# Delta rule and mixture of a six-stage decoder: when small triangular inverses are turned between layouts, and how keys and norms are interleaved

## The reference

```python
combine = combine.at[jnp.arange(N)[:, None], topk_idx].add(topk_scores)
hidden = silu(einsum('nd,kde->nke', flat, gate)) * einsum('nd,kde->nke', flat, up)
out = einsum('nk,nkd->nd', combine, einsum('nke,ked->nkd', hidden, down))
out = out + (silu(flat @ sh_gate.T) * (flat @ sh_up.T)) @ sh_down.T
```

```python
K = K / max(norm(K), EPS); beta = sigmoid(x @ Wbeta + b_beta)
def step(W, inp):
    pred = einsum('bhij,bhj->bhi', W, k_t)
    W_new = W + b_t * einsum('bhi,bhj->bhij', v_t - pred, k_t)
    return W_new, einsum('bhij,bhj->bhi', W_new, q_t)
```

## Time and profile before

| what | value |
|---|---|
| median of 3 runs | 1878.89 us |
| lowest, highest | 1873.01, 1880.94 us |
| the profiled execution | 1880.19 us, its span 1878.4 us |
| busy share of the span | PE 86%, DVE 62%, ACT 49%, POOL 34% |
| mean granted clock of PE | 0.914 of full speed |
| mixture, about | 990 to 1185 us of the span |
| delta rule, about | 1185 to 1700 us |

### The profile page before, as it was taken

One profiled execution on the slowest core, in us unless ns is written; L12 is line 12 of the kernel. 1 busy time (PEld: TensorE's weight loads), 2 busy tenths in 40 slices (PEclk: granted clock), 3 DMA queues, 4 the chain that ended last, 5 costly groups with the idle time before them and its releaser, 6 DMA issues.

```text
span 1878.4 us, 41473 instructions
## 1 busy us (share of the span) xinstructions
PE 1622.5 (86%) x17930; PEld 847.8 (45%) x17930; DVE 1168.0 (62%) x2285; ACT 912.0 (49%) x1263; POOL 646.1 (34%) x696
## 2 busy tenths in 40 slices
PE   4888887778998999899888987898988889878995
PEld 1222222223334334333434544676767778664443
DVE  6778775776575665657516567456464665455655
ACT  1665564456875775677571332344444443223120
POOL 1000000245654664565470007545665456000000
PEclk8897898899999999999997998799998999977898
DMA  3000002222242222242301000000000000100000
GB/s 138 1 1 1 1 1 76 65 66 66 80 105 66 77 80 66 66 105 77 80 10 60 3 1 1 13 14 14 3 14 14 14 14 21 47 2 1 6 6 12
DMA packets 31271, 69.91 MB, mean 37 GB/s; under 512 B 4954, under 2 KB 6047, under 8 KB 30832
## 3 DMA queue, kind: packets, MB, share of 16 engines
q1 hardware_dynamic: 31088, 67.26, 12.4%
HBM read 46.73 MB, written 20.51 MB: 36 GB/s over the span
## 4 chain that ended last, share of the span: by engine, by line
PE 65%; DVE 25%; issue 5%; ACT 4%; DMA 1%; POOL 1%; SPq 0%; DVEq 0%; ACTq 0%
PE ps L158 63%; DVE a_MX L362 4%; DVE b_mx L826 2%; DVE st L164 1%; PE ps L218 1%; DVE sq L197 1%; DVE st L190 1%; DVE d_G L1550 1%; DVE st L201 1%; DVE b_rd L988 1%; DVE st L179 1%; DVE d_XE L1556 1%; DVE b_VL L773 1%; POOL b_EL L898 1%; DVE a_QS L164 1%
## 5 line engine op out<-in xcount | busy, mean ns | idle before, releaser
L898 POOL TENSOR_TENSOR b_EL<-b_X,b_EH 128x1024 f16<-128x1024 f32 x160 | 341.1, 2132 | 318.6 <-ACT b_EH L161 318.4
L826 DVE TENSOR_REDUCE b_mx<-ps 128x2 f32<-128x666 f32 x256 | 217.2, 848 | 127.8 <-PE ps L158 127.7
L1603 POOL TENSOR_TENSOR d_tmp<-d_G,d_XI 128x31 f32<-128x31 f32 (+15 forms) x248 | 126.6, 510 | 321.2 <-DVE d_G L1550 194.8
L880 ACT ACTIVATE b_X<-ps 128x1024 f32<-128x1024 f32 x160 | 163.8, 1024 | 123.0 <-PE ps L158 120.6
L161 ACT ACTIVATE b_EH<-b_X 128x1024 f16<-128x1024 f32 x160 | 169.2, 1058 | 27.6 <-PE ps L158 16.7
L399 ACT ACTIVATE a_E<-ps 128x1024 f32<-128x1024 f32 x128 | 131.2, 1025 | 103.2 <-PE ps L158 103.1
L158 PE MATMUL ps<-b_M,b_S 128*128 128x512 f16 (+1 forms) x768 | 179.4, 388 | 2.2 <-ACT b_X L880 2.1
L362 DVE TENSOR_REDUCE a_MX<-ps 128x2 f16<-128x1024 f32 x128 | 155.0, 1226 | 40.8 <-PE ps L158 40.8
L1606 POOL TENSOR_TENSOR d_XI<-d_XI,d_tmp 128x31 f32<-128x31 f32 (+15 forms) x248 | 137.5, 554 | 19.4
L158 PE MATMUL ps<-b_Hk,b_Hq 64*128 64x333 f16 x512 | 83.6, 323 | 45.3 <-DVE b_mx L826 40.0
L381 POOL TENSOR_TENSOR a_QS<-a_QS,a_MR 128x512 f16<-128x512 f16 x16 | 18.5, 1158 | 273.5 <-ACT a_MR L161 273.5
(11 more groups left out here) (317 smaller groups left out, 3349.7 us busy)
## 6 DMA issues: line engine op xcount, KB each, us to landing
b_S<-s_xk SPq DMA_DIRECT2D x48, 336.0 KB, 6.3
b_M<-s_xq SPq DMA_DIRECT2D x48, 256.0 KB, 5.0
s_xk<-b_Hk SPq DMA_DIRECT2D x16, 336.0 KB, 2.2
s_xk<-b_Lk SPq DMA_DIRECT2D x16, 336.0 KB, 2.5
s_xq<-b_Hq SPq DMA_DIRECT2D x16, 256.0 KB, 2.0
s_xq<-b_Lq SPq DMA_DIRECT2D x16, 256.0 KB, 2.0
d_XI<-eye SPq DMA_DIRECT2D x8, 512.0 KB, 3.6
f_w<-f_w SPq DMA_DIRECT2D x1, 2048.0 KB, 8.4
```

The costliest lines, as they stand in the source:

```text
L826: v.e.tensor_reduce(out, PS[:, bk:bk + 2, 0:333], AX, ALU.max).then_inc(sem("b_mx"), 1)
L880: a.e.activation(b_X[k % 2], PS[:, bk:bk + 2, :], ACT.Exp, scale=0.125).then_inc(sem("b_ex"), 1)
L898: last = p.e.tensor_tensor(b_EL[k % 6], b_X[k % 2], b_EH[k % 6], ALU.subtract)
L1603: e.tensor_tensor(tm, a, x, ALU.mult).then_inc(*p.step())
```

## The change

Five things are edited. The computation stays.

1. `d_keys_*` is split into `d_rows_*` (17 steps: products, squares, scalings) and `d_turn_*` (6 steps: turns and key products, which now stand at its steps 2 and 5 where they stood at 2 and 4). In the mixture rows(1) and turn(1) become a third stream, beside rows(0), turn(0) and the blocks of m = 0.
2. Every norm of the mixture is `fine`, and the expert steps take three steps of it at p = 2 and two at p = 3 to 6, where they took one at p = 2 to 5.
3. `d_XE` is cleared at the start of the mixture. It moves to another address, and it now waits for readers in stage B instead of for the mixture's last `down`.
4. Each 128 x 1024 transpose of DVE becomes two of 16 of the 32 rows or columns (512 elements per partition). Back for m stands late in the even unit ahead, the blocks of m + 1 in halves in the odd unit.
5. Between mixture and delta rule, back(0) and blocks(1) are woven with `last_c` and prep(0), where `swap(0)` ran ahead of both.

```diff
-            if b and 1 < p < 6:
-                next(rest, None)
+            if b and 1 < p < 7:
+                for _ in range(3 if p == 2 else 2):
+                    next(rest, None)
...
-            yield from normalize(v, xb(b), 1e-5, "xr_C", fine=b == NB - 1)
+            yield from normalize(v, xb(b), 1e-5, "xr_C", fine=True)
...
+            clear(lane)
             weave((route(lane, 0), 1))
             weave((tail, 23), (experts(lane, 0), 9))
             weave((experts(lane, 1), 9))
-            weave((both(experts(lane, 2), experts(lane, 3)), 18), (both(keys0, both(blocks(lane), keys1)), 2 * D_KEYS + 8))
+            weave((both(experts(lane, 2), experts(lane, 3)), 18),
+                  (both(rows(lane, 0), later(6, both(turn(lane, 0), blocks(lane)))), 62),
+                  (later(12, both(rows(lane, 1), later(5, turn(lane, 1)))), 41))
             last(lane, NB - 1)
-            clear(lane)
...
-            v.wait_ge("c_dm", 4)
+            v.wait_ge("b_sc", 11 * NU)
+            v.wait_ge("b_mt", 16 * NU)
+            v.wait_ge("b_r", 96 * NU)
+            v.wait_ge("b_mr", 16 * NU)
             v.e.memset(d_XB, 0.0).then_inc(sem("d_zv"), 1)
...
-                if p in (2, 4):
-                    j, n = p // 2 - 1, 2 * m + p // 2 - 1
+                if p in (2, 5):
+                    j, n = p // 3, 2 * m + p // 3
...
-        def d_blocks_vector(v, m):
+        def d_blocks_vector(v, m, half):
             v.wait_ge("d_lc", m + 1)
             v.wait_ge("d_inv", m)
-            v.e.transpose(d_G.rearrange("p t s -> p s t"), d_L[m % 2][:, :, 32:64].rearrange("p t s -> p s t")).then_inc(sem("d_gt"), 1)
+            r = slice(16 * half, 16 * half + 16)
+            v.e.transpose(d_G[:, :, r].rearrange("p t s -> p s t"),
+                          d_L[m % 2][:, :, 32:64][:, :, r].rearrange("p t s -> p s t")).then_inc(sem("d_gt"), 1)
...
+        def d_back_vector(v, m, half):
             v.wait_ge("d_zv", 1)
             v.wait_ge("d_inv", m + 1)
             v.wait_ge("d_um", 8 * m)
-            v.e.transpose(d_XB[:, :, 32:64].rearrange("p i t -> p t i"), d_XI.rearrange("p s t -> p t s")).then_inc(sem("d_xt"), 1)
+            r = slice(16 * half, 16 * half + 16)
+            v.e.transpose(d_XB[:, :, 32:64][:, :, r].rearrange("p i t -> p t i"),
+                          d_XI[:, :, r].rearrange("p s t -> p t s")).then_inc(sem("d_xt"), 1)
...
+        def d_back_steps_vector(v, m):
+            for half in range(2):
+                d_back_vector(v, m, half)
+                yield
+                yield
...
+        def d_blocks_steps_vector(v, m):
+
+            yield
+            for half in range(2):
+                d_blocks_vector(v, m, half)
+                yield
+                yield
+                yield
...
-            run(swap(lane, 0))
-            weave((prep(lane, 0), 17), (last_c(lane), 14))
+            weave((last_c(lane), 18), (prep(lane, 0), 17), (both(back(lane, 0), blocks(lane, 1)), 24))
...
-                if u % 2 and u < 15:
-                    streams.append((swap(lane, u // 2 + 1), 24))
+                if u % 2 and u // 2 + 2 < NH:
+                    streams.append((blocks(lane, u // 2 + 2), 24))
+                if u % 2 == 0 and u < 12:
+                    streams.append((later(20, back(lane, u // 2 + 1)), 24))
+                if u == 13:
+                    streams.append((back(lane, 7), 24))
```

More of the change, by code:

```diff
@@ L1348, in c_down_vector, with c_order @@
             v.wait_ge("c_add", b + 1)
-            yield from normalize(v, xb(b), 1e-5, "xr_C", fine=b == NB - 1)
-        def c_order(lane, route, experts, tail, keys0, keys1, last, clear, blocks):
+            yield from normalize(v, xb(b), 1e-5, "xr_C", fine=True)
+        def c_order(lane, route, experts, tail, rows, turn, last, clear, blocks):
+            clear(lane)
             weave((route(lane, 0), 1))
@@ L1443, in d_keys_tensor, with d_turn_tensor @@
                 yield
-            for _ in range(17):
-                yield
-            for p in range(5):
+            yield from later(D_ROWS - 4, ())
+        def d_turn_tensor(t, m, banks):
+            e, KV, KT = t.e, d_KV[m % 3], d_KT[m % 2]
+            for p in range(6):
                 if p < 4:
@@ L1484, in d_keys_scalar, with d_turn_scalar @@
                 yield
-            for _ in range(17):
-                yield
-            for p in range(5):
+            yield from later(D_ROWS - 4, ())
+        def d_turn_scalar(a, m):
+            e, KT = a.e, d_KT[m % 2]
+            for p in range(6):
                 if p < 4:
@@ L1494, in d_keys_scalar, with d_rows_vector @@
                 yield
-        def d_keys_vector(v, m):
-            e, b, i = v.e, m // 2, m % 4
-            KV, L = d_KV[m % 3], d_L[m % 2]
+        def d_rows_vector(v, m):
+            e, b, i, KV = v.e, m // 2, m % 4, d_KV[m % 3]
             v.wait_ge("ld_w3", 144)
@@ L1523, in d_keys_vector, with d_turn_vector @@
                 yield
-            for _ in range(4):
-                yield
-            for p in range(5):
-                if p in (2, 4):
-                    n = 2 * m + p // 2 - 1
+        def d_turn_vector(v, m):
+            e, L = v.e, d_L[m % 2]
+            for p in range(6):
+                if p in (2, 5):
+                    n = 2 * m + p // 3
                     v.wait_ge("d_gm", n + 1)
@@ L1535, in d_keys_vector, with d_keys @@
                 yield
+        def d_keys(lane, rows, turn, m, *banks):
+            yield from rows(lane, m, *banks)
+            yield from later(4, ())
+            yield from turn(lane, m, *banks)
         def d_blocks_scalar(a, m):
@@ L1570, in d_first_vector @@
             yield
-            d_blocks_vector(v, 0)
-            yield
+            for half in range(2):
+                d_blocks_vector(v, 0, half)
+                yield
         def d_first_scalar(a):
@@ L1914, in build, with d_order @@
         D_LATE = {5: 0, 9: 1, 12: 2}
-        def d_order(lane, chain, prep, keys, late, first, attend, split, last_c, swap):
-            run(swap(lane, 0))
-            weave((prep(lane, 0), 17), (last_c(lane), 14))
+        def d_order(lane, chain, prep, keys, late, first, attend, split, last_c, back, blocks):
+            weave((last_c(lane), 18), (prep(lane, 0), 17), (both(back(lane, 0), blocks(lane, 1)), 24))
             cross = e_stream(lane, first, attend)
```

64 lines of the change are left out of this document (31 added, 33 removed).

## The result

The changed kernel takes 1847.56 us (median of 4 runs, 1843.07 to 1853.16), the kernel before in the same comparison 1875.95 us (4 runs, 1866.07 to 1880.94). The ratio is 0.988, with a 95% interval from 0.983 to 0.992, so it is faster by 0.8 to 1.7%. The forecast was 1851 us, with a range from 1836 to 1870. In later comparisons the kernel before had medians of 1868.3 (19 runs), 1870.2 (7) and 1873.0 (9), and the changed kernel had 1846.3 us (4 runs). The gain is thus 28.4 us in this comparison and 21 to 27 us by the later ones.

The account below looks back on a forecast made before the run. PE, busy for 86% of the span, was the bound, so time could come only from its waits and low-clock stretches. Mixture 9, seam 3, odd units 10, clock 9, less 2, make 29: 1880.19 - 29 = 1851 us, range 1836 to 1870.

Parts of the forecast that it names:

- Clear at no cost: Clearing `d_XE` moves to where DVE waits for PE 1.75 us; costs nothing, or 1.8 us if that stretch is filled.
- Mixture, 9 us (4.8 of gaps, 4.2 of clock): Mixture: 4.8 us from PE's turns of keys starting sooner, 4.2 from slow stretches; 9 us, from 2 to 12.
- the step that gives the 4.8: Mixture: fewer DVE operations ahead of the fourth `d_KV` scaling, so PE turns keys 2.4 us sooner in each of two batches.
- The rival that the order on a full DVE gives nothing: Mixture: DVE is at 93%, so order only shifts waits; 1860 us (1856 to 1866), chance 0.10.
- Seam, 3 us: Mixture to delta rule: corner products sooner, bound by ACT's copies of `d_XE`; 3 us, from 1 to 5.
- Odd units, gaps 10 less 2 for new waits: Delta rule: six gaps before `d_S` additions shrink, 10 us (7 to 12); new waits in even units cost 2 (0 to 6).
- the 2 us charged for them: Even units: 1 us for late halves waiting on the inverse, 1 for reordered ACT copies and PE products; from 0 to 6.
- Clock, 9 us of 18.7: Behind the six odd-unit seams: half of the 18.7 us lost to low clock returns; 9 us, from 2 to 15.
- the rival that all comes back: Mixture and odd-unit seams: all the clock returns, 18.7 us instead of 9 at the seams; 1838 us (1832 to 1843), chance 0.12.
- The premise of that half: PE's gaps: 1.12 us or less bring no clock drop, six of 2.7 or more do; the new 1.5 us lies between.
- POOL: Delta rule, rival: DVE waits for POOL's inverses; the gain is gone when each ends some 7 us later; chance 0.11.

Follow-up runs that it names:

- the shorter inverses: The changed kernel with 7 of the 31 pairs of each POOL inverse left out, so the output is incomplete: 1836.6 us in one execution.
- The longer ones: The changed kernel with every second product of each POOL inverse done twice, 8 us longer, same result: 1897.0 us in one execution.

## Why the prediction was right, step by step

- **Clear at no cost.** It left the path. From the first routing product to the first `down` the four profiles with the old place took 47.6 to 48.9 us, the ten with the new one 45.6 to 47.3. Just ahead of that product PE waits for `c_oh` for 4.23 us in the changed kernel where it waited for 3.91, so the clear costs 0.3 us at its new place at most. The clear was not moved by itself.
- **Mixture, 9 us (4.8 of gaps, 4.2 of clock).** Measured 11.8 from second to fourth `down`: PE's idle time falls from 20.2 to 12.1 us, by 8.2, and its busy time by 3.5. The forecast of 9 came near, in part by luck, since the step that gives the 4.8 was not what happened. I said that the turn of the keys comes 2.3 us sooner. The scalings do end 2.6 sooner, but PE turns the keys where it did, and the gain comes from key products of m = 1 that fill the gap. I counted these as moved, not as filling. The rival that the order on a full DVE gives nothing is refuted for this stretch by its length in every kernel with both edits.
- **Seam, 3 us.** 2.6 (15.3 for 18.0) in both profiles of the changed kernel and in every other that leaves the seam and the inverses as they are, and the binding wait is the one that was named, ACT's copies of `d_XE`.
- **Odd units, gaps 10 less 2 for new waits.** PE's idle time from corner to `e_mrf` is 37.1 to 39.0 us in the three profiles of the kernel before (39.0 is 397.78 less 358.74), and 33.8 and 30.2 in the two of the changed kernel: 3 to 9 us less. The single gaps were right, 1.29 to 1.55 for a forecast of about 1.5, and they are 10 us shorter together. Some of that comes back as other waits, as the 2 us charged for them say in kind, though it can be more than 2.
- **Clock, 9 us of 18.7.** PE's busy time in the same stretch was 358.7 to 364.2 us in the three profiles of the kernel before and is 348.2 and 351.0 now: 8 to 16 us less, and the mean clock rises from 0.91 to 0.93 to 0.97. The run with whole transposes shows that this hangs on the gap: at 2.2 us the slow stretches are back, at 1.3 to 1.5 most are gone. But the 9 came out near by two errors that offset each other. I took half of the slow time behind the seams to come back, and 31 to 34 of 37.5 us came back. I took each us of it to cost half a us, and it costs about 0.3: over the whole stretch the slow time falls from 57 to 71 us to 19 to 26, by some 40, and PE's busy time by some 12 (an estimate from the means of these five profiles). So in the clock itself the rival that all comes back was nearer than the forecast.
- **The premise of that half.** I wrote that gaps of 1.12 us and less are followed by no drop, gaps of 2.7 by one, and that nothing lies between. Its first and last part are wrong in the trace of the kernel before. Stages A and B alone have some thirty gaps between, some with a drop behind them and some without, and inside unit 0 a drop of 6.8 us follows gaps of 0.79 and 0.94 (a row of PE's timeline, then the window behind it; three such places):

```profile
274.66 0.66 PE L218 MATMUL ps<-ident,a_oq 128*128 128x128 f32 x4 [1.81 <-DVE a_oq L432]
278.10:284.90 6.80, 6.80 (x19) 4.34 (x20) 5.54 (x6) 0.65 (x1) 0.00 (x0) 0.50 0.00 0
...
575.45 0.60 PE L158 MATMUL ps<-b_rp,b_sel 128*128 128x512 f16 x2 [1.55 <-DVE b_den L959]
575.40:582.20 6.80, 6.75 (x51) 3.35 (x52) 1.87 (x4) 4.50 (x5) 3.20 (x3) 1.00 0.01 2
...
1212.03 0.46 PE L158 MATMUL ps<-d_PT,d_UW 64*64 64x64 f32 x14 [0.94 <-issue]
1214.10:1220.90 6.80, 6.80 (x17) 4.51 (x16) 1.35 (x3) 2.67 (x6) 6.09 (x10) 0.50 0.00 0
```

- **POOL.** The rival didn't come, by a thin margin: a wait of 9.4 us in three turns back (4.60 of it at the seam, 4.07 in unit 13), of which the shorter inverses give 3 us back. The longer ones cost 37 us for 8, more than the whole gain, so the point that decides lies below 8 us. In proportion it is near 6 (an estimate from this one point and a gain of 28 us), where I wrote 7.
- **The sum.** The parts that repeat add up to 11.8 + 2.6 + 16 to 20 = 30 to 34 us, with up to 2 more ahead of the first `down`, and the medians of runs show 21 to 28. So the places and the waits were right, and the total came out partly because errors offset each other: the mixture's step, the two halves of the clock's term, and what was gained and doesn't reach the end. Part of that loss is the stretch from `e_mrf` to F: 107 to 110 us in the kernel before, 110 to 123 in the changed one, and 123 in those two profiles where the late last inverse leaves PE a gap of 2.3 us and half rate follows at once. The rest is open: the mixture's edits alone gain 11.5 us in their stretch and 4 us between the medians of 10 runs and 19, and I found no place where they lose the rest.

## What to carry to other kernels

When one execution scatters by more than the effect, cut the profiles at the same instructions and compare the windows: in the mixture they repeat within 0.1 us and carry a reading that totals can't, and in the delta rule within 4 us, still less than the gain there. A transposition that isn't urgent is worth moving or halving less for its own microsecond than for what the clock does behind the gap: here six gaps shortened from 2.2 to 1.5 us made their stretch 12 us shorter, 10 of them less busy time of PE. A rule drawn from a few gaps of one trace (no drop below 1.1 us, a drop above 2.7) should be held against all gaps of that trace first. And before a side engine's result is asked for earlier, measure how much longer its work may become before it binds.
